# The second edge stage of a fused graph and feed-forward kernel: 98 unrolled tiles become 14 unrolled tiles and three laps of 28, with 42 row buffers

## What is computed

```
h = (x @ W.T).reshape(n, 8, 64)
e = leaky_relu(sum(h[src] * a_src) + sum(h[dst] * a_dst), 0.2)      # 8 numbers an edge
e = e * (1.0 + et_emb[edge_type]) * edge_weight[:, None]
e_max = zeros((n, 8)).at[dst].max(e)
e = exp(e - e_max[dst])
e_sum = zeros((n, 8)).at[dst].add(e)
alpha = e / (e_sum[dst] + 1e-10)
msg = h[src] * alpha[:, :, None]
out = zeros((n, 8, 64)).at[dst].add(msg).reshape(n, 512) + x
return layer_norm(out) * ln_gamma + ln_beta
```

## Time and profile before

| | us |
|---|---|
| median of three runs | 1786.2 |
| profiled execution, device time | 1774.8 |
| its span | 1773.1 |
| TensorE busy | 1651.2 (93%) |
| VectorE busy | 884.8 (50%) |
| GpSimd busy | 647.0 (36%) |
| edge stage of L2, first gather to last use | about 1082 to 1261 |

### The profile page before, as it was taken

The page is one execution under the profiler, slowest core; times in us unless marked ns, Lnnn a source line. Parts: engine busy times, 40 slices in busy tenths (PEclk is TensorE's granted clock), DMA queues, the critical chain, the costliest instruction groups (busy, mean ns, idle before and its releaser), DMA issues.

```text
span 1773.1 us, 23528 instructions
## 1 busy us (share of the span) xinstructions
PE 1651.2 (93%) x7277; PEld 934.7 (53%) x7307; DVE 884.8 (50%) x2162; ACT 500.7 (28%) x1586; POOL 647.0 (36%) x756
## 2 busy tenths in 40 slices
PE   6989999999898999999999998697899999999898
PEld 4634444445755646555556666442444555555555
DVE  8878887878835453344354157785523101111322
ACT  1124444447431413223231125110200111111234
POOL 5868788773232333333441814566200000000000
PEclk9999999999899999999998998899899999999999
DMA  8030101105413223222316744455326121310020
GB/s 317 1 104 25 60 25 30 50 14 133 128 48 129 78 82 91 58 82 64 83 38 139 267 146 144 136 149 162 105 72 218 61 88 47 101 62 22 6 67 18
DMA packets 119614, 161.76 MB, mean 91 GB/s; under 512 B 49497, under 2 KB 61721, under 8 KB 119154
## 3 DMA queue, kind: packets, MB, share of 16 engines
q1 hardware_dynamic: 93056, 115.43, 20.9%
q0 software_dynamic: 18592, 29.91, 6.3%
q10 hardware_dynamic: 7890, 15.44, 2.6%
HBM read 145.26 MB, written 15.47 MB: 91 GB/s over the span
## 4 chain that ended last, share of the span: by engine, by line
PE 81%; DVE 8%; DMA 4%; issue 3%; POOL 2%; ACT 2%; ACTq 0%; another core or an unknown queue 0%; DVEq 0%; POOLq 0%; SPq 0%
PE psum L374 79%; DMA arena<-tab_h,sd_t 1%; POOL ring L631 1%; DVE stats L471 1%; DMA ring<-tab_h,sd_t 1%; DVE ring L1306 1%; DVE xn L2074 0%; PE psum L1034 0%; DVE xn L2080 0%; DMA xT<-tab_h,sd_t 0%; POOL arena L631 0%; DVE xn L2093 0%; ACT xT L415 0%; DMA x<-in_x 0%; PE psum L405 0%
## 5 line engine op out<-in xcount | busy, mean ns | idle before, releaser
L374 PE MATMUL psum<-arena 128*128 128x384 f32 (+9 forms) x1804 | 313.8, 328 | 18.8 <-DVE arena L670 5.6
L374 PE MATMUL psum<-arena,ring 128*128 (+1 forms) x1478 | 321.2, 362 | 9.6 <-issue 6.2
L374 PE MATMUL psum<-xT,ring 128*128 128x384 f32 x928 | 308.7, 493 | 7.9 <-ACT xT L415 4.2
L374 PE MATMUL psum<-ring,arena 128*128 128x512 f32 (+1 forms) x570 | 263.0, 608 | 11.2 <-DVE ring L670 6.6
L374 PEld LDWEIGHTS psum<-arena 128*128 128x128 f32 (+5 forms) x1804 | 193.1, 152 | 148.0 <-issue 74.5
L374 PE MATMUL psum<-ring,xT 128*128 128x512 f32 x552 | 249.8, 605 | 1.3 <-issue 0.7
L374 PEld LDWEIGHTS psum<-xT,ring 128*128 128x128 f32 x928 | 177.0, 192 | 133.1 <-issue 16.3
L374 PEld LDWEIGHTS psum<-arena,ring 128*128 128x128 bf16 (+1 forms) x1504 | 137.5, 113 | 130.4 <-issue 29.3
L1085 ACT ACTIVATE ring<-ring 128x128 f32<-128x128 f32 x416 | 123.3, 297 | 173.3 <-DVE ring L1372 173.3
L374 PEld LDWEIGHTS psum<-ring,arena 128*128 128x128 f32 (+1 forms) x570 | 99.9, 188 | 134.9 <-issue 133.9
L374 PEld LDWEIGHTS psum<-ring,xT 128*128 128x128 f32 x552 | 104.3, 194 | 122.2 <-issue 119.3
(11 more groups left out here) (481 smaller groups left out, 1739.4 us busy)
## 6 DMA issues: line engine op xcount, KB each, us to landing
ring<-in_L_ffn_w SPq DMA_DIRECT2D x22, 1024.0 KB, 7.3
ring<-in_L_gnn_m_w SPq DMA_DIRECT2D x8, 1024.0 KB, 5.8
ring<-in_L_ffn_expert_weights SPq DMA_DIRECT2D x8, 1024.0 KB, 5.7
ring<-tab_key ACTq DMA_DIRECT2D x24, 256.0 KB, 3.1
ring<-in_L_gnn_Wv SPq DMA_DIRECT2D x5, 1024.0 KB, 5.1
tab_w<-xn SPq DMA_DIRECT2D x6, 768.0 KB, 14.9
ring<-in_L_gnn_Ww SPq DMA_DIRECT2D x4, 1024.0 KB, 17.3
ring<-in_L_gnn_wq SPq DMA_DIRECT2D x4, 1024.0 KB, 5.5
```

The costliest lines, as they stand in the source:

```text
L374: return nc.tensor.matmul(o, a, b, start=start, stop=stop)
```

## The change

- `GR` is 42. The first 14 buffers are used once; tiles from 14 on go round through the other 28 (`AGAIN`). So tile T from 42 on needs the buffer of tile T - 28, and GpSimd's wait names that tile. The three new buffers are a new tile `row_more` and two pieces of arena; for tiles 40 and 41 GpSimd waits until tile 0 has been used.
- GpSimd's full waits at 72, 84 and 96 are gone; those at 48 and 60 and the ones below 39 stay, and so does the limit of four underway. GpSimd's own code is still unrolled.
- On TensorE and VectorE tiles 14 to 97 are a loop of three laps of 28 tiles. Waits there compare with a register, and the columns of the weight tables and of `chunk2_i` are addressed through registers. ScalarE is as before.
- Landings raise one of seven semaphores of their own (`h_row_in`) in place of one of eight shared ones.
- At the start of the program the nine fp32r matmuls and VectorE's cast are gone, and `keep_clock` issues six matmuls of 128x256 in place of three.

```diff
-GR = 39
+GR = 42
...
-        zeros_r = sb("zeros_r", [P, 512], mybir.dt.float32r)
...
+        row_more = sb("row_more", [P, D])
...
-        go_rows += [xn2[:, t, :] for t in range(NT)]
+        go_rows += [xn2[:, t, :] for t in range(NT)] + [row_more[:], view(11216, D), view(11216 + D, D)]
         assert len(go_rows) == GR
+        FIRST = 2 * RB
+        AGAIN = GR - FIRST
+        LAPS = (TT2 - FIRST) // AGAIN
...
-        ROW_GROUP, LOOP_GROUP = 6, 12
...
+        ROW_GROUP, IN_LOOP = 6, (48, 60)
+
+        def row_landed(eng, T, lap=None):
+
+            eng.wait_ge(h_row_in[T % RB], 16 * (T // RB + 1) + (0 if lap is None else lap * (16 * AGAIN // RB)))
+
+        def row_of(T):
+            return go_rows[T if T < FIRST else FIRST + (T - FIRST) % AGAIN]
...
                 if T >= GR:
-                    pool.wait_ge(msg_used, T - GR + 1 + 2 * RB)
-                if T > 0 and T % (ROW_GROUP if T < GR else LOOP_GROUP) == 0:
+                    pool.wait_ge(msg_used, T - AGAIN + 1 + 2 * RB)
+                elif T >= GR - 2:
+                    pool.wait_ge(msg_used, 1 + 2 * RB)
+                if T in IN_LOOP or (0 < T < GR and T % ROW_GROUP == 0):
                     for k in range(max(T - ROWS_UNDERWAY, 0), T):
                         row_landed(pool, k)
                 elif T >= ROWS_UNDERWAY:
                     row_landed(pool, T - ROWS_UNDERWAY)
...
+            for T in range(FIRST):
+                message(T)
+            with od.loop(LAPS, 3 * AGAIN // (2 * RB)) as lap:
+                for T in range(FIRST, GR):
+                    message(T, lap)
...
+            with pe.Fori(0, LAPS) as lap:
+                four = chunks_of(AGAIN * lap + FIRST)
+                for k in range(AGAIN):
+                    summed(FIRST + k, four[k % 4], lap)
+                    if k % 4 == 3 and k + 1 < AGAIN:
+                        four = chunks_of(AGAIN * lap + FIRST + k + 1)
...
             b = banks.open(pe, "bucket")
-            for w in (512, 512, 512, 256, 256, 256, 128, 128, 128):
-                mm(b[:, 0:w], zeros_r[:, 0:P], zeros_r[:, 0:w], True, True)
-            keep_clock(b, 3)
+            keep_clock(b, 6)
             pe.wait_ge(bucket_ready, 1)
...
-            V.tensor_copy(zeros_r[:], zeros[:])
```

More of the change, by code:

```diff
@@ L657, in dve_hot_rows, with message @@
                                     ALU.is_equal).then_inc(hot_rows, 1)
         def dve_scatter_rows(dve, od):
-            for T in range(TT2):
+            def message(T, lap=None):
+                at = T if lap is None else T + AGAIN * lap
                 if T % RB == 0 and T > 0:
[L663 to L670, removed]
+                    dve_hot_rows(dve, T // RB, lap)
+                row_landed(dve, T, lap)
+                rows_of = row_of(T).rearrange("p (h d) -> p h d", h=H8)
+                nc.vector.tensor_tensor(rows_of, rows_of, w_tile[:, :, bass.ds(at, 1)].broadcast_to([P, H8, HD]),
@@ L686, in chunks_of @@
             _, some = nc.values_load_multi_w_load_instructions(
-                chunk2_i[0:1, T:min(T + 4, TT2)], engines=[mybir.EngineType.PE], min_val=0, max_val=NT - 1,
+                chunk2_i[0:1, slice(T, min(T + 4, TT2)) if isinstance(T, int) else bass.ds(T, 4)], engines=[mybir.EngineType.PE], min_val=0, max_val=NT - 1,
                 skip_runtime_bounds_check_because="a sum of two comparisons is 0, 1 or 2")
@@ L703, in pe_scatter_rows, with summed, after @@
             none = zeros[:].bitcast(BF16)
-            four = chunks_of(0)
-            for T in range(TT2):
+            def summed(T, cd, lap=None):
+                def after(n, per):
+                    return n if lap is None else n + lap * (AGAIN // per)
                 onto = hot[:, T // RB % 2, T % RB, :]
                 if T % RB == 0:
-                    pe.wait_ge(hot_rows, T // RB + 1)
-                pe.wait_ge(msg_ready, T + 1)
-                cd = four[T % 4]
-                mm(wide[:, bass.ds(cd * 512, D)], onto, go_rows[T % GR], False, False)
+                    pe.wait_ge(hot_rows, after(T // RB + 1, RB))
+                pe.wait_ge(msg_ready, after(T + 1, 1))
+                mm(wide[:, bass.ds(cd * 512, D)], onto, row_of(T), False, False)
                 if T % RB == 0:
-                    pe.wait_ge(bf16_made, len(UNITS) + T // RB + 1)
+                    pe.wait_ge(bf16_made, after(len(UNITS) + T // RB + 1, RB))
                 if T % (2 * RB) == 0:
-                    pe.wait_ge(pieces_made, len(UNITS) + T // (2 * RB) + 1)
+                    pe.wait_ge(pieces_made, after(len(UNITS) + T // (2 * RB) + 1, 2 * RB))
                 mm(wide[:, bass.ds(cd * 3 * H8 + SUMS * 512, 3 * H8)], hot_half[:, T // RB % 2, T % RB, :],
-                   w_pieces[:, T, :, :].rearrange("p k h -> p (k h)"), False, False).then_inc(msg_used, 1)
-                if T % 4 == 3 and T + 1 < TT2:
-                    four = chunks_of(T + 1)
+                   w_pieces[:, bass.ds(after(T, 1), 1), :, :].rearrange("p t k h -> p (t k h)"), False, False).then_inc(msg_used, 1)
+            four = chunks_of(0)
+            for T in range(FIRST):
+                summed(T, four[T % 4])
+                if T % 4 == 3:
+                    four = chunks_of(T + 1)
+            with pe.Fori(0, LAPS) as lap:
[4 more added lines that the diff above has]
+                        four = chunks_of(AGAIN * lap + FIRST + k + 1)
             bk = [psum[:, c, :] for c in range(SUMS + 1)]
```

24 lines of the change are left out of this document (13 added, 11 removed).

## The result

The changed kernel took 1796.7 us (median of 20 runs, 1786.0 to 1809.1), the kernel before 1786.3 us (20 runs, 1783.4 to 1795.2). The ratio is 1.0053, 95% interval 1.0036 to 1.0071: slower by half a per cent, where I had said faster. The profiled execution of the changed kernel is one of its longest, 1808.9 us, with a span of 1807.1 us against 1773.1.

What follows compares the result with a forecast made beforehand. It took TensorE to bound the edge stage's tiles 0 to 57 and GpSimd's gathers the rest. Terms -9.2 + 0.4 - 0.9 + 0.2 - 0.1 = -9.6 us took 1786.2 to 1776.6 us, range 1770 to 1788.

Steps and rivals of the forecast that it cites:

- the sum's last lines: Whole kernel: terms sum to -9.6 us; the median's 11.4 us above the profiled execution is kept, giving 1776.6 us.
- Rival F: Timed runs against profile: the gain doesn't carry over whole; half of it, -4.5 us, 1782 us; chance 0.09.
- Full waits, 9.2 us: GpSimd's gathers at tiles 72, 84 and 96: ordinary steps replace three full waits, 9.2 us gained.
- Meetings with VectorE: Gathers beside VectorE's one-hot build and weight split: two that met the stall now slow gathers, 0.4 us given back.
- The last tile, 0.9 us: TensorE's end of the edge stage: last tile at full speed, VectorE's wait for weights gone, 0.9 us gained.
- Loop on TensorE, 0: TensorE's edge-stage tiles: register work and loop heads, 1.5 us, hidden behind the gathers; charge 0.
- on VectorE, 0.2: VectorE's edge-stage loop: register work hidden, loop exit and one address at the end cost 0.2 us, bounds 0 and 0.5.
- Buffers, 0: GpSimd's wait for tile T - 28 from tile 42 on: tile 14 used in time, 3.6 us to spare, charge 0.
- the cover: Edge stage: 11 us between TensorE's own end and the gathers' end, hiding up to 0.13 us a tile over 84 tiles.
- Start, 0.1 us: Program start: the fillers and wait before the bucket matmul end sooner, 0.1 us gained, bounds 1 us either way.
- The slower rival, E: TensorE's loop: 0.51 us paid at every tile, 42.8 us over 84; +21.5 us, 1807.7 us; chance 0.05.

Runs made afterwards that it cites:

- e10: The changed kernel run again, with its own profile, against the kernel before: 1794.3 us, ratio 1.0046.
- e11: The changed kernel with the loops on TensorE and VectorE written out, reuse after 28 tiles kept, against the kernel before: 1786.5 us, ratio 0.9993.
- e12: The changed kernel with both loops written out and the 42 buffers used in turn, against the kernel before: 1792.1 us, ratio 1.0018.
- e9: The kernel before, unchanged, with a profile of its own: 1788.2 us in its series, its single own run 1783.1 us.
- e14: The changed kernel run again in another series, against the kernel before: 1767.8 us, ratio 0.9947.
- e13: The changed kernel with both loops in two laps of 42 tiles and buffers used in turn, against the kernel before: 1767.5 us, ratio 0.9950.
- e1: The changed kernel with GpSimd's full waits at 72, 84 and 96 put back, against the kernel before: 1777.4 us, ratio 1.0002.
- e4: The kernel before with only the start of the program changed, against the kernel before: 1776.7 us, ratio 1.0002.
- e3: The kernel before with only the full waits at 72, 84 and 96 removed, against the kernel before: 1767.3 us, ratio 0.9948.
- e16: The kernel before without the full waits at 72, 84 and 96, repeated in another series, against the kernel before: 1768.2 us, ratio 0.9945.
- e18: The kernel before without the full waits at 72, 84 and 96, repeated once more, against the kernel before: 1767.0 us, ratio 0.9938.
- e5: The changed kernel with the loop kept on TensorE only and VectorE's tiles written out, against the kernel before: 1790.7 us, ratio 1.0004.

## Why the prediction was wrong

The step that failed is in the sum's last lines: "The median of the runs is 11.4 us above it; with the same difference the forecast is ..." The profile had been taken on a chip of the early kind, and the 20 runs of the result, like those of the kernel before beside them, by their times on one of the late kind. Those 11.4 us were no constant to be added. They are for the most part the late first product (78.8 against 59.6 us; the stage 190.0 against 179.6, 10.4 us longer), and it moves which wait comes last. Rival F named the gap and put it at half of the gain; it never asked what a later start would do to the new buffer plan. On a late chip the two terms that I had charged with nothing or next to it, the buffers and the loops, took the gain and more: the loops' 7.7 us stand in the times (e10 against e11), and e11, which has the reuse and no loop, is level with the kernel before. That the reuse is what it lost there is read from GpSimd's stream, and e12's time doesn't bear it out. In profiles, e10's sum of weights stands 5.1 us later than e9's, where the sum had it 9.6 earlier: 2.4 us in GpSimd's stream, where the reuse took 8.5 and two full waits less gave 5.9, and 2.7 us behind the last gather.

- **Full waits, 9.2 us.** Right on early chips: alone they gave 9.6, 9.5 and 11.2 us. On late ones GpSimd's stream shows nearly the same size (2.97 us for each wait less; the buffers in turn end it 8.4 us sooner), but no time there confirms it.
- **Meetings with VectorE, 0.4 us given back.** Small, as put: 1.41 us a step in e9 and e12, 1.42 in e14, against my 1.405.
- **The last tile, 0.9 us.** Right where nothing else is late (e14: 1.13 us, no wait for the weights in place of 0.95). On late chips some of the changed kernel's tiles run at half speed in front of the end instead.
- **Loop on TensorE, 0, and on VectorE, 0.2.** Right on early chips: e13's tiles show no issue gap at all, e1's 0.2 us, and e1 is at 1.0002. On late chips this term was mis-sized: e10 against e11 is 1794.3 against 1786.5, 7.7 us (3.4 in their profiles, at the sum of weights), and I had bounded VectorE's loop at 0.5. I asked only whether register work fits under the cover, and took for granted that each engine goes on as soon as its waits are met.
- **Buffers, 0, "3.6 us are to spare".** The way of working was right and its input was not. (It also counted a tile too many: 1143.24 is the start of tile 1, so tile 14 is used at 1143.24 + 14 x 0.973 = 1156.9, and some 5 us were to spare.) In e10 tile 1 starts at 1160.35, so tile 14 is used at 1174.0, while GpSimd wants its buffer at 1162.9: 11.1 us short, and 11.49 were measured. A margin of 4 to 5 us stood on a start that varies by 20.
- **Start, 0.1 us.** No difference (e4).
- **The slower rival, E,** put 0.51 us on each of TensorE's tiles. That isn't what happened: in the result's profile tiles 14 to 60 ran 0.97 us apart, the heads of laps one and two among them.

The Trainium skill, Runtime: NRT & Kernel Launch, section Instruction fetch mechanics, says that a taken branch to a target outside what is held forces a fetch. No run here shows whether a lap's head is held. If it weren't, the returns to it would show gaps, and the rule alone doesn't explain the traces: e13 with its two laps shows no issue gap in the whole stage, and in the result's profile one gap, 4.40 us, stands at the third head, but none at the second, and those of 2.14 to 3.98 us stand inside the lap.

**What stays open.** Why TensorE and VectorE idle on some chips, with their waits met, in the stretch in which gathers run (late instructions are a guess that no view shows), and whether it is the chip; what exactly the loop on VectorE adds there; whether the 8.5 us of the reuse would show in the times of a late chip; and whether buffers in turn with loops (e13) or the waits alone (e3) keep their gain on a late chip, since neither ran on one. On early chips the waits alone do all the good (e3, e16, e18), which no larger kernel bettered.

## What to carry to other kernels

Compare the profiled execution with the timed runs before anything is summed: where they differ by more than the effect in question, find the stretch that differs, or cost the change for both. A margin between a wait and its release is worth as much as the start it is counted from; ask what it becomes when the stage in front slips by as much as the profile and the median differ. Where buffers are reused sooner than in turn, count how many are free when the consumer starts late, and where a ratio is under a per cent, time on more than one chip.

## What the hardware showed

- The series, each on another chip as far as is known, differ in one stretch. The kernel before reaches its stage's first product 59.6 us after the first gather in one profile and 78.8 in the other, with 8.2 (e4, which differs in its start only) against 27.4 us (e9) of weight loads waiting on issue, and its median is 1777 to 1778 or 1786 to 1790.
- The granted clock can fall while TensorE is busy. In e12 TensorE was busy for all of three stretches of 10 us from 1296.9 on, and the granted clock was 1.00, 0.76 and 0.89.
- A gather that starts while VectorE runs f32 products back to back can last far longer than 0.95 us, and most don't. In e10 VectorE was busy without a pause longer than 0.13 us through 1174.37 to 1182.87, the 8.50 us of tile 42's gather, and that gather ended within the second cast (its timeline):

```profile
1175.96 4.30 DVE L678 TENSOR_TENSOR ring<-ring,arena 128x512 f32<-128x512 f32 x7
1180.17 1.09 DVE L666 TENSOR_TENSOR arena<-iota,ranking 128x896 f32<-128x896 f32 x1
1181.18 0.69 DVE L678 TENSOR_TENSOR ring<-ring,arena 128x512 f32<-128x512 f32 x1
1181.78 0.26 DVE L682 CAST arena<-arena  x1
1182.08 0.36 DVE L683 TENSOR_TENSOR arena<-arena 128x112 f32 x1
1182.57 0.33 DVE L684 CAST arena<-arena 128x112 f32 x1
```

  In e9 and e12 the gather ended in the same cast, which then took 0.44 and 0.45 us. In e5 and e11 it ended after 6.5 us, at the one-hot build. The Trainium skill, SBUF — State Buffer, section Who interferes with whom, says that a VectorE instruction with two SBUF inputs contends with a GpSimd instruction that reads SBUF. A gather reads its row numbers, `sd_t`, there. The long gathers agree; but the four right behind the long one in e10 took 0.95 to 0.97 us beside the same kind of products (from 1183.17 on), and in e9 those of tiles 39 to 47, ahead of the long one, 0.94 to 1.47, which that rule alone doesn't explain.
